# Rounded halves in the expert tiles, first scores moved into the projections, transposes moved up behind the scores

## The chip, the cores and the metric

One Trainium2 chip, of which the kernel uses one core in one launch. The metric is the device time of a launch in microseconds (us). TensorE (PE) multiplies, VectorE (DVE) and GpSimd (POOL) work elementwise and along rows, ScalarE (ACT) evaluates functions and copies, and SyncE (SP) starts DMAs. They run side by side and wait for each other through semaphores.

## The reference

A decoder of two layers runs over `x` (16 batches of 112 rows, width 256) with a context of 16 times 375 rows. Each layer is attention, attention on the context, and a feed-forward part with experts, each with a layer norm ahead and the input added. Everything is float32.

```python
# layer 0
scores = einsum('bhtd,bsd->bhts', q, k1) * scale        # 8 heads of 128, one k and v
probs = softmax(where(causal, scores, finfo.min)); out = (probs @ v1) @ Wo.T
...
q = ln_lat @ Wq; kv = concat([xn, ln_lat]) @ Wkv        # cross attention: 16 heads of 64, 375 + 112 keys
weight = softmax(where(full_mask, einsum('bhld,bhnd->bhln', q * scale, k * scale), neg)); out = (weight @ v) @ Wout
...
expert_idx = argmax(softmax(x @ Wr.T))                  # 8 experts, one per row
inter = gelu(x @ W1[e] + b1[e]); y = inter @ Wo + bo + x; out = layer_norm(y) * gamma + beta
# layer 1
... 16 heads of 64, one k and v, causal; layer_norm(x) times gamma ahead
ctx = (Q @ K.T / dk) @ V                                # context mix: no softmax, so K.T @ V can be made first
x = layer_norm(residual + ctx @ wo + wo_b) * ln_g + ln_b
topv, topi = top_k(softmax(x @ Wg + bg), 2)             # 4 experts, low-rank changes of one shared layer
h = relu(x @ Wi + lora); out = sum_e w_e * (h_e @ Wo)
```

## The kernel before, in words

The order of the work on every engine is written out by hand. Each stage is a block with one function per engine; a semaphore is raised by an instruction when it ends and waited for on the engine that needs it, and each engine takes its instructions strictly in the written order. Nothing moves across the end of a block. Tiles have the stage as a prefix: `l0q`/`l0a` (first attention: projections, then the loop over batches), `l0x` (cross attention), `l0f` (experts of layer 0), `l1a`, `l1x` (context mix), `l1f`.

**l0a.** Projections run in four groups of four batches: eight query products, each in three passes of rounded halves (hi times hi, lo times hi, hi times lo, type fp32r), then k and v. Then, in a new block, each batch goes through `score` on PE (one 112x112 product per head), `softmax` on DVE (add the causal mask, row maximum, shift), `exp` on ACT with the row sums, `invert_sums` on DVE, the division on POOL (`pn`), `transpose_p` on PE, `copy_pT`, `weigh_values`, and `project_out`. The scores of batches 0 and 1 open the block.

**l0x.** A loop over 16 batches, each in eight steps of two heads (`over_steps`: batches 1 to 14 share one loop body). In a step PE makes the scores of its heads from 64 rows of the array (`score`), projections of k and v for later steps or for the next batch, the transposes of the probabilities of the step before (`transpose_p`), and their product with v (`weigh_values`). DVE masks the scores (`mask_score`), copies half of the transposes, inverts the sums, subtracts rounded from full values (the lo halves). ACT does the exponentials, the other half of the copies and the rounded hi halves. POOL divides the probabilities in place.

**l0f.** Rows are routed to experts by a scatter of DMAs on POOL, ahead of which products for the later context mix (`gram`) are made. Then 21 tiles of 128 sorted rows run: `expand` (32 products of 128 columns), gelu on ACT into `hT` (two buffers), and `contract` on PE, 16 products of 256 columns in float32 with `wo`, of width 256, which is resident. Each tile loads 1 MB of weights, three tiles ahead. DVE and POOL normalise the tile's output.

**l1a** is as `l0a` with 16 heads in two halves, k; its block opens with the scores of batch 0 (both halves) and of batch 1. **l1x** takes four groups of four batches: normalise on ACT, transposes, a product with wq, one with the mix of each batch, and one with wo on PE; on DVE the output's statistics, `update` (L2271) and the row statistics; POOL adds biases and takes powers (`add_bias`, `invert_output`). `find_best` on DVE and `subtract_first` on POOL choose the experts of a group two groups later; those of group 2 end the block. **l1f** begins with the transposes of `one_hot` (L2664).

## Time and profile before

| | us |
|---|---|
| median of 3 runs | 1776.1 |
| lowest, highest | 1771.97, 9249.27 |
| profiled execution, its own time | 1779.62 |
| its span, first to last instruction | 1777.8 |

The mean granted clock of TensorE is 0.973 of full speed.

| engine | busy us | share |
|---|---|---|
| PE | 1671.7 | 94% |
| DVE | 1022.1 | 57% |
| ACT | 750.2 | 42% |
| POOL | 530.4 | 30% |

Stages by the timeline: first attention's projections to 74.6 us and its loop to about 211; cross attention about 228 to 1058; routing and first context products to 1111; expert tiles to 1269; context products to 1335; second attention's projections to 1402 and its loop to 1558; context mix to 1640.6; last experts to 1778. A row of the timeline gives the start, the time from start to end of a run of like instructions, the engine, the line, the operation, out<-in, shapes and the count; in brackets stands how long the engine had idled before and what it waited for. Ends of matmuls are modelled, so distances between starts are the safer measure of PE.

### The profile page before, as it was taken

The page shows a single profiled execution, that of the slowest core. Times are in us where ns is not written, and L with a number is a line of the kernel's source. Part 1 is how long each engine was busy: PE and PEld are TensorE (multiplying, and loading weights), DVE is VectorE, ACT ScalarE, POOL GpSimd, SP SyncE. Part 2 cuts the span into 40 slices and gives each one's busy share as a digit, 9 for nine tenths or more (in the row PEclk, how much of TensorE's full clock was granted, in tenths as well). Part 3 has the DMA queues.
Part 4 walks back from the last instruction along what each step waited for, and adds up shares of the span by engine and source line. Part 5 has one row for each costly group of instructions (what it writes and reads, how often), then busy time and mean ns, then how long its engine had stood idle before and what let it go on. Part 6 is the DMA issues. An engine that isn't in the chain of part 4 may idle for free. (4 is left out here: it accounts for less than half of the span.)

```text
span 1777.8 us, 32493 instructions
## 1 busy us (share of the span) xinstructions
PE 1671.7 (94%) x11198; PEld 1323.0 (74%) x11198; DVE 1022.1 (57%) x2461; ACT 750.2 (42%) x2126; POOL 530.4 (30%) x579
## 2 busy tenths in 40 slices
PE   7899899999999999999999987999988799977998
PEld 6687677777777777777777766889877677655666
DVE  5466466655666666566666554142264388757574
ACT  2255344444444444444444430343203477642221
POOL 1022223333333333333333324243420133444000
PEclk9999999999999999999999998999998899987999
DMA  3100300000000000000002004765210000020000
GB/s 99 57 1 1 105 20 11 11 10 10 1 9 10 10 10 10 10 4 6 10 10 63 0 20 154 201 223 187 90 41 20 1 1 1 2 58 1 11 11 21
DMA packets 48805, 67.41 MB, mean 38 GB/s; under 512 B 11826, under 2 KB 42770, under 8 KB 46034
## 3 DMA queue, kind: packets, MB, share of 16 engines
q1 hardware_dynamic: 47186, 62.66, 11.5%
q0 software_dynamic: 1536, 3.67, 0.6%
q8 instruction: 49, 0.80, 0.2%
q14 instruction: 34, 0.28, 0.1%
HBM read 57.02 MB, written 9.31 MB: 37 GB/s over the span
## 5 line engine op out<-in xcount | busy, mean ns | idle before, releaser
L697 POOL TENSOR_TENSOR l0x_p<-l0x_p,l0x_inv 112x488 f32<-112x488 f32 x256 | 251.8, 1005 | 472.6 <-DVE l0x_inv L791 472.6
L900 ACT ACTIVATE l0x_p<-l0x_s,l0x_low 112x488 f32<-112x488 f32 x256 | 178.3, 697 | 275.1 <-DVE l0x_low L780 274.6
L780 DVE CUSTOM_DVE_ANT_0 l0x_s<-l0x_score_ps,l0x_bias 112x488 f32<-112x488 f32 x256 | 160.1, 662 | 113.9 <-PE l0x_score_ps L1040 104.4
L767 DVE TENSOR_TENSOR l0x_kT_lo<-l0x_proj_ps,l0x_kT_hi 128x488 fp32r<-128x488 f32 x128 | 85.3, 667 | 106.3 <-ACT l0x_kT_hi L890 106.3
L1061 PEld LDWEIGHTS l0x_oT_ps<-l0x_pT,l0x_v 122*64 122x64 f32 x2048 | 100.7, 138 | 43.9 <-issue 32.6
L1061 PE MATMUL l0x_oT_ps<-l0x_pT,l0x_v 122*64 122x112 f32 x2048 | 127.9, 267 | 4.9 <-DVE l0x_pT L786 4.1
L1048 PE MATMUL l0x_pT_ps<-ident,l0x_p 112*122 112x112 f32 x1024 | 120.2, 260 | 0.4 <-POOL l0x_p L697 0.3
L1048 PEld LDWEIGHTS l0x_pT_ps<-ident,l0x_p 112*122 112x122 f32 x1024 | 107.0, 138 | 18.2 <-issue 6.0
L996 PE MATMUL l0x_proj_ps<-l0x_kvT_hi,l0x_wkv_hi 128*128 128x488 f32 x256 | 111.0, 434 | 2.9 <-DVE l0x_kvT_lo L755 2.9
L1904 POOL TENSOR_TENSOR l1a_pn<-l1a_p,l1a_inv 112x896 f32<-112x896 f32 x32 | 53.9, 1684 | 190.6 <-DVE l1a_inv L1933 190.6
L1989 ACT ACTIVATE l1a_p<-l1a_p,l1a_shift 112x112 f32<-112x112 f32 x256 | 95.4, 374 | 32.4 <-DVE l1a_shift L1927 32.4
L1005 PE MATMUL l0x_proj_ps<-l0x_wkv_hi,l0x_kvT_hi 128*122 128x512 f32 x256 | 107.0, 418 | 0.0
L1006 PE MATMUL l0x_proj_ps<-l0x_wkv_lo,l0x_kvT_hi 128*122 128x512 f32 x256 | 101.1, 395 | 0.0
L1007 PE MATMUL l0x_proj_ps<-l0x_wkv_hi,l0x_kvT_lo 128*122 128x512 f32 x256 | 101.1, 395 | 0.0
L997 PE MATMUL l0x_proj_ps<-l0x_kvT_lo,l0x_wkv_hi 128*128 128x488 f32 x256 | 99.2, 388 | 0.0
L998 PE MATMUL l0x_proj_ps<-l0x_kvT_hi,l0x_wkv_lo 128*128 128x488 f32 x256 | 99.2, 388 | 0.0
L890 ACT ACTIVATE l0x_kT_hi<-l0x_proj_ps 128x488 fp32r<-128x488 f32 x128 | 72.8, 569 | 35.7 <-PE l0x_proj_ps L998 35.7
L786 DVE COPY l0x_pT<-l0x_pT_ps 122x448 f32<-122x448 f32 x128 | 79.0, 617 | 9.9 <-PE l0x_pT_ps L1048 9.6
L1661 PE MATMUL l0f_hT_ps<-l0f_xsT,l0f_w 128*128 128x128 f32 x672 | 78.5, 275 | 0.0
L1661 PEld LDWEIGHTS l0f_hT_ps<-l0f_xsT,l0f_w 128*128 128x128 f32 x672 | 76.8, 192 | 0.1
L1672 PE MATMUL l0f_y_ps<-l0f_wo,l0f_hT 128*128 128x256 f32 x336 | 75.8, 379 | 0.0
L996 PEld LDWEIGHTS l0x_proj_ps<-l0x_kvT_hi,l0x_wkv_hi 128*128 128x128 f32 x256 | 48.7, 190 | 29.4 <-issue 21.7
(371 smaller groups left out, 3685.8 us busy)
## 6 DMA issues: line engine op xcount, KB each, us to landing
l0f_w<-in_l0f_w SPq DMA_DIRECT2D x21, 1024.0 KB
l0x_c_in<-in_ctx SPq DMA_DIRECT2D x16, 375.0 KB
l1x_gram_context<-in_ctx SPq DMA_DIRECT2D x16, 375.0 KB
sorted_x<-l0x_zeros SPq DMA_DIRECT2D x1, 2816.0 KB, 15.3
l0f_xs<-sorted_x SPq DMA_DIRECT2D x21, 128.0 KB, 2.1
sorted_y<-l0f_ys SPq DMA_DIRECT2D x21, 128.0 KB, 1.7
l0x_wkv<-in_l0x_wkv SPq DMA_DIRECT2D x2, 1024.0 KB, 9.0
x<-in_x SPq DMA_DIRECT2D x4, 448.0 KB, 8.9
```

The costliest lines, as they stand in the source:

```text
L697: nc.gpsimd.tensor_tensor(p[:, i % 2, a, :], p[:, i % 2, a, :], inv[:, i % 2, a:a + 1].broadcast_to([S, KEYS]), ALU.mult).then_inc(pn_read ...
L780: nc.vector.tensor_tensor_reduce(s_sb[:, h % 2, :], score_ps[0:S, h % 2, 0:KEYS], bias[:], -SCALE, 3.4e38, ALU.add, ALU.min, low[:, h:h + ...
L900: nc.scalar.activation(p[:, h // 2 % 2, h % 2, :], s_sb[:, h % 2, :], ACT.Exp, scale=-1.0, bias=low[:, h:h + 1], accum_out=total[:, h:h + ...
L996: nc.tensor.matmul(out, wkv_hi[:, c, at], kvT_hi[:, c, :], start=(c == 0), stop=False)
L997: nc.tensor.matmul(out, wkv_hi[:, c, at], kvT_lo[:, c, :], start=False, stop=False)
L998: done = nc.tensor.matmul(out, wkv_lo[:, c, at], kvT_hi[:, c, :], start=False, stop=(c == KC - 1))
L1005: nc.tensor.matmul(out, kvT_hi[:, c, keys], wkv_hi[:, c, at], start=(c == 0), stop=False)
L1006: nc.tensor.matmul(out, kvT_hi[:, c, keys], wkv_lo[:, c, at], start=False, stop=False)
L1007: done = nc.tensor.matmul(out, kvT_lo[:, c, keys], wkv_hi[:, c, at], start=False, stop=(c == KC - 1))
L1048: done = nc.tensor.transpose(pT_ps[0:KT, a, t * S:(t + 1) * S], p[:, i % 2, a, t * KT:(t + 1) * KT], ident[0:S, 0:S])
L1061: done = nc.tensor.matmul(oT_ps[a * DH:(a + 1) * DH, 0, (i % 4) * S:(i % 4 + 1) * S], v[:, t, (2 * i + a) * DH:(2 * i + a + 1) * DH], pT[: ...
L1661: done = nc.tensor.matmul(hT_ps[:, 2 * (i % 2) + f // 4, (f % 4) * 128:(f % 4 + 1) * 128], w1[:, i % 3, c, f * 128:(f + 1) * 128], xsT[:, ...
```

## The change

1. **First attention:** the scores of batches 0 and 1 are made by PE within the last group of query products (ahead of the first and the fifth product), and batch 0 goes through softmax, exponentials and inversion there; its division opens POOL's next block.
2. **Cross attention:** on PE the transposes of the step before come directly behind the scores. On DVE the copy of the transposes and the inversion come ahead of the splits of queries, values, inputs and keys; on ACT the second exponential and the copy come ahead of the rounding.
3. **Experts of layer 0:** gelu's output goes into one buffer (in the place of `gram_k`), is rounded on ACT (`hT_hi`) and subtracted on DVE (`hT_lo`); `wo` is loaded first and split into halves once (ACT, POOL). `contract` is now 24 products of type fp32r and 256 columns. The third set of expert weights is loaded only when `wo_lo` is made, since `wo` lies in its buffer. The output is scaled in place.
4. **Second attention:** scores of batch 0 move ahead of the last group's query products, with mask, maximum, exponentials and inversion between the copies. `p` becomes two tiles. `wo` is loaded when the loop's block begins. ACT normalises the first four batches for the context mix at the end.
5. **Context mix:** that normalising is gone from its start; POOL adds the next group's bias ahead of `invert_output`; `find_best` and `subtract_first` of group 2 move into the last stage, behind the first result.

What PE's order is at three places, the lines being those of each kernel. Before, the end of the projections of the first attention (`l0q`) and the start of its loop (the three rows of an `L333`-`L335` product stand once):

```order
L333 MATMUL l0a_o_ps<-l0q_xT_hi,l0q_wq_hi 128x448
L334 MATMUL l0a_o_ps<-l0q_xT_lo,l0q_wq_hi 128x448
L335 MATMUL l0a_o_ps<-l0q_xT_hi,l0q_wq_lo 128x448
L343 MATMUL l0a_o_ps<-l0q_xT,l0q_wk 128x448 x2
L347 MATMUL l0a_o_ps<-l0q_wv,l0q_xT 112x128 x8
L180 UNCONDITIONAL_BRANCH
L476 UNCONDITIONAL_BRANCH
L482 MATMUL l0a_score_ps<-l0a_kT,l0a_qT 112x112 x16
L491 MATMUL l0a_score_ps<-ident,l0a_pn 112x112 x8
L500 MATMUL l0a_o_ps<-l0a_pT,l0a_v 128x448 x2
```

After, from the fifth query product of the last group to its sixth, and the end with the start of the loop:

```order
L387 MATMUL l0a_o_ps<-l0q_xT_hi,l0q_wq_hi 128x448
L388 MATMUL l0a_o_ps<-l0q_xT_lo,l0q_wq_hi 128x448
L389 MATMUL l0a_o_ps<-l0q_xT_hi,l0q_wq_lo 128x448
L185 MATMUL l0a_score_ps<-l0a_kT,l0a_qT 112x112 x8
L387 MATMUL l0a_y_ps<-l0q_xT_hi,l0q_wq_hi 128x448
```

And after, the end of that group and the start of the loop:

```order
L389 MATMUL l0a_o_ps<-l0q_xT_hi,l0q_wq_lo 128x448
L397 MATMUL l0a_o_ps<-l0q_xT,l0q_wk 128x448 x2
L401 MATMUL l0a_o_ps<-l0q_wv,l0q_xT 112x128 x8
L221 UNCONDITIONAL_BRANCH
L497 UNCONDITIONAL_BRANCH
L503 MATMUL l0a_score_ps<-ident,l0a_pn 112x112 x8
L512 MATMUL l0a_o_ps<-l0a_pT,l0a_v 128x448 x2
L185 MATMUL l0a_score_ps<-l0a_kT,l0a_qT 112x112 x8
```

Scores now stand in front of the fifth product, and the loop's block opens with the transposes of `l0a_pn`, 8 of them, instead of 16 score products.

In the cross attention, before, the step with keys 0 and 1 of the next batch (scores, one k product of six, transposes, the next):

```order
L1036 MATMUL l0x_score_ps<-l0x_kT_hi,l0x_q_hi 112x488 x2
L1038 MATMUL l0x_score_ps<-l0x_kT_lo,l0x_q_hi 112x488 x2
L1040 MATMUL l0x_score_ps<-l0x_kT_hi,l0x_q_lo 112x488 x2
L996 MATMUL l0x_proj_ps<-l0x_kvT_hi,l0x_wkv_hi 128x488
L997 MATMUL l0x_proj_ps<-l0x_kvT_lo,l0x_wkv_hi 128x488
L998 MATMUL l0x_proj_ps<-l0x_kvT_hi,l0x_wkv_lo 128x488
L996 MATMUL l0x_proj_ps<-l0x_kvT_hi,l0x_wkv_hi 128x488
L997 MATMUL l0x_proj_ps<-l0x_kvT_lo,l0x_wkv_hi 128x488
L998 MATMUL l0x_proj_ps<-l0x_kvT_hi,l0x_wkv_lo 128x488
L1048 MATMUL l0x_pT_ps<-ident,l0x_p 122x112 x8
L996 MATMUL l0x_proj_ps<-l0x_kvT_hi,l0x_wkv_hi 128x488
```

After:

```order
L1046 MATMUL l0x_score_ps<-l0x_kT_hi,l0x_q_hi 112x488 x2
L1048 MATMUL l0x_score_ps<-l0x_kT_lo,l0x_q_hi 112x488 x2
L1050 MATMUL l0x_score_ps<-l0x_kT_hi,l0x_q_lo 112x488 x2
L1058 MATMUL l0x_pT_ps<-ident,l0x_p 122x112 x8
L1006 MATMUL l0x_proj_ps<-l0x_kvT_hi,l0x_wkv_hi 128x488
L1007 MATMUL l0x_proj_ps<-l0x_kvT_lo,l0x_wkv_hi 128x488
L1008 MATMUL l0x_proj_ps<-l0x_kvT_hi,l0x_wkv_lo 128x488
```

The transposes moved from behind the first k product to ahead of it.

In a tile, before:

```order
L1650 MATMUL l0f_xT_ps<-ident,l0f_xs 128x128 x2
L1661 MATMUL l0f_hT_ps<-l0f_xsT,l0f_w 128x128 x16
L1672 MATMUL l0f_y_ps<-l0f_wo,l0f_hT 128x256 x8
L1650 MATMUL l0f_xT_ps<-ident,l0f_xs 128x128 x2
L1661 MATMUL l0f_hT_ps<-l0f_xsT,l0f_w 128x128 x16
```

After (the three rows of a pass repeat eight times):

```order
L1686 MATMUL l0f_xT_ps<-ident,l0f_xs 128x128 x2
L1697 MATMUL l0f_hT_ps<-l0f_xsT,l0f_w 128x128 x16
L1709 MATMUL l0f_y_ps<-l0f_wo_hi,l0f_hT_hi 128x256
L1710 MATMUL l0f_y_ps<-l0f_wo_lo,l0f_hT_hi 128x256
L1711 MATMUL l0f_y_ps<-l0f_wo_hi,l0f_hT_lo 128x256
```

Each float32 product became three of type fp32r.

The diff, cut:

```diff
@@ l0_attention: score, softmax, exp, normalise now stand ahead of the projections @@
+                normalise(pool, 0)
...
+                        if q == Q - 1 and i == 1:
+                            dve.wait_ge(late_w, 32)
+                            softmax(dve, 0)
+                        elif q == Q - 1 and i == 5:
+                            invert_sums(dve, 0)
+                softmax(dve, 1)
...
+                        if q == Q - 1 and i == 0:
+                            score(pe, 0)
+                        elif q == Q - 1 and i == 4:
+                            score(pe, 1)
@@ l0_cross_attention, DVE @@
                     mask_score(b, 2 * i + 1)
+                    if i >= 1:
+                        copy_pT(b, i - 1)
+                    elif not first:
+                        copy_pT(b - 1, HP - 1)
+                    invert_totals(b, i)
                     if i == 0:
                         split_queries(b, 1)
-                        if not first:
-                            copy_pT(b - 1, HP - 1)
...
-                    if i >= 1:
-                        copy_pT(b, i - 1)
-                    invert_totals(b, i)
@@ ACT @@
                     exp(b, 2 * i)
-                    if i == 0:
-                        round_queries(b, 1)
-                    elif i >= 4 and not last:
-                        round_keys(b + 1, 2 * i - 8)
...
                     exp(b, 2 * i + 1)
...
+                    if i == 0:
+                        round_queries(b, 1)
+                    elif i >= 4 and not last:
+                        round_keys(b + 1, 2 * i - 8)
@@ PE @@
                     score(b, i)
...
+                    transpose_p(b, i - 1)
                     if i <= 2:
                         project_high_v(b, 2 * i - 1)
                     elif i >= 4 and not last:
                         project_k(b + 1, 2 * i - 8)
...
-                    transpose_p(b, i - 1)
@@ l0_experts @@
+        wo_hi, wo_lo = ph.sb("wo_hi", [128, FC, D], F32R), ph.sb("wo_lo", [128, FC, D], F32R)
+        wo = w1[:, 2].rearrange("p c (g n) -> p (c g) n", n=D)
...
+                if i == 2:
+                    sp.wait_ge(wo_lo_ready, 2)
...
+            def split_tile(i):
+                for n in range(2):
+                    part = slice(n * FC // 2, (n + 1) * FC // 2)
+                    dve.wait_ge(hT_hi_ready, 2 * i + n + 1)
+                    nc.vector.tensor_tensor(hT_lo[:, i % 2, part], hT[:, part], hT_hi[:, i % 2, part].bitcast(F32),
+                                            ALU.subtract).then_inc(hT_lo_ready, 1)
...
+                    hi, lo = hT_hi[:, i % 2, f, :], hT_lo[:, i % 2, f, :]
+                    nc.tensor.matmul(y_ps[:, i % 2, 0:D], hi, wo_hi[:, f, :], start=(f == 0), stop=False)
+                    nc.tensor.matmul(y_ps[:, i % 2, 0:D], hi, wo_lo[:, f, :], start=False, stop=False)
+                    done = nc.tensor.matmul(y_ps[:, i % 2, 0:D], lo, wo_hi[:, f, :], start=False, stop=(f == FC - 1))
@@ l1_attention @@
+                        if q == Q - 1 and i == 1:
+                            mask_scores(dve, 0, 0, p_even)
+                            find_shift(dve, 0, 0, p_even)
+                            mask_scores(dve, 0, 1, p_even)
+                        elif q == Q - 1 and i == 3:
+                            find_shift(dve, 0, 1, p_even)
+                        elif q == Q - 1 and i == 5:
+                            invert_sums(dve, 0, 0)
+                        elif q == Q - 1 and i == 7:
+                            invert_sums(dve, 0, 1)
...
+                        if q == Q - 1 and i == 0:
+                            exp(act, 0, range(0, 8), p_even)
+                        elif q == Q - 1 and i == 2:
+                            exp(act, 0, range(8, 16), p_even)
...
+                    if q == Q - 1:
+                        pe.wait_ge(act_step, in_step(q, 2))
+                        score(pe, 0, 0)
+                        score(pe, 0, 1)
...
+            def _(sp):
+                sp.dma_start(wo[:], A["l1a_wo"].rearrange("(h p) n -> p h n", p=128)).then_inc(wo_w, 16)
@@ l1_context_mix @@
-                invert_output(g)
                 if g + 1 < G:
                     add_bias(g + 1)
+                invert_output(g)
...
-            subtract_first(G - 2)
...
-            find_best(G - 2)
...
-            normalise(0)
@@ l1_experts, DVE @@
                 if g == 0:
-                    find_best()
+                    find_best(0, G - 2)
+                    find_best(1, G - 1)
```

## Rows read from the trace of the kernel before

**Rows 1.** Stretches: length; PE, PEld, DVE, ACT, POOL busy (count); PE clock; DMA share; GB/s.

```profile
300.00:350.00 50.00, 49.99 (x372) 39.13 (x371) 30.77 (x80) 24.41 (x57) 16.82 (x18) 1.00 0.03 9
1200.00:1250.00 50.00, 50.00 (x348) 46.87 (x347) 12.88 (x28) 18.70 (x63) 19.00 (x34) 1.00 0.57 188
1559.60:1600.00 40.40, 32.40 (x137) 22.93 (x138) 22.39 (x54) 20.51 (x34) 20.79 (x28) 0.78 0.22 64
```

**Rows 2.** What TensorE waited for, whole run: us in total, times, longest.

```profile
PE l1x_o_ps L2403 <- DVE l1x_y L2221: 7.2, 3, 3.2
...
PE l1f_first_hot_ps L2664 <- PEq L2135: 3.9, 1, 3.9
...
PE l1x_xT_ps L2375 <- ACT l0f_x L2308: 3.3, 1, 3.3
```

**Rows 3.** Timeline, start of the first attention: start, us, engine, line, form, count.

```profile
74.61 3.37 PE L482 MATMUL l0a_score_ps<-l0a_kT,l0a_qT 128*112 128x112 f32 x32 [1.47 <-PEq L180]
84.03 1.74 PE L491 MATMUL l0a_score_ps<-ident,l0a_pn 112*112 112x112 f32 x8 [6.05 <-POOL l0a_pn L367]
91.52 0.93 PE L491 MATMUL l0a_score_ps<-ident,l0a_pn 112*112 112x112 f32 x8
```

**Rows 4.** Timeline, TensorE and GpSimd, cross attention of one batch, two steps.

```profile
350.94 0.47 PE L1036 MATMUL l0x_score_ps<-l0x_kT_hi,l0x_q_hi 64*112 64x488 f32 x2
351.79 0.98 PE L1048 MATMUL l0x_pT_ps<-ident,l0x_p 112*122 112x112 f32 x8
352.61 3.62 PE L1070 MATMUL l0x_proj_ps<-l0x_wout,l0x_oT 128*112 128x256 f32 x16
...
350.13 1.96 POOL L697 TENSOR_TENSOR l0x_p<-l0x_p,l0x_inv 112x488 f32<-112x488 f32 x2 [3.51 <-DVE l0x_inv L791]
...
363.89 0.48 PE L1036 MATMUL l0x_score_ps<-l0x_kT_hi,l0x_q_hi 64*112 64x488 f32 x2
364.74 0.49 PE L996 MATMUL l0x_proj_ps<-l0x_kvT_hi,l0x_wkv_hi 128*128 128x488 f32 x1
366.18 0.93 PE L1048 MATMUL l0x_pT_ps<-ident,l0x_p 112*122 112x112 f32 x8
366.88 0.47 PE L996 MATMUL l0x_proj_ps<-l0x_kvT_hi,l0x_wkv_hi 128*128 128x488 f32 x1
368.30 0.40 PE L1005 MATMUL l0x_proj_ps<-l0x_wkv_hi,l0x_kvT_hi 128*122 128x512 f32 x1
```

**Rows 5.** Timeline, expert tiles: TensorE from one tile to the next.

```profile
1201.06 3.74 PE L1661 MATMUL l0f_hT_ps<-l0f_xsT,l0f_w 128*128 128x128 f32 x32
1204.63 3.62 PE L1672 MATMUL l0f_y_ps<-l0f_wo,l0f_hT 128*128 128x256 f32 x16
1208.09 0.38 PE L1650 MATMUL l0f_xT_ps<-ident,l0f_xs 128*128 128x128 f32 x2
```

**Rows 6.** Groups by form: weight loads of the experts; one rounding on ScalarE.

```profile
L1661 PEld LDWEIGHTS l0f_hT_ps<-l0f_xsT,l0f_w 128*128 128x128 f32 x425 | 48.6, 192 | 0.0
...
L876 ACT ACTIVATE l0x_kvT_hi<-l0x_kvT 128x488 fp32r<-128x488 f32 x1 | 0.6, 612 | 0.3 <-DVE l0x_kvT L748 0.3
```

**Rows 7.** The page's group of the exponentials, and the timeline, start of the second attention.

```profile
L1989 ACT ACTIVATE l1a_p<-l1a_p,l1a_shift 112x112 f32<-112x112 f32 x256 | 95.4, 374 | 32.4 <-DVE l1a_shift L1927 32.4
...
1403.10 1.28 ACT L1989 ACT_TABLE_LOAD   x1 [0.27 <-PEq L1775]
...
1407.68 1.04 PE L2019 MATMUL l1a_score_ps<-l1a_kT,l1a_qT 64*112 64x112 f32 x16 [1.28 <-DVE l1a_p L1917]
1414.16 1.71 PE L2031 MATMUL l1a_score_ps<-ident,l1a_pn 112*112 112x112 f32 x8 [5.43 <-POOL l1a_pn L1904]
```

**Rows 8.** Timeline, context mix: VectorE's update beside GpSimd and alone.

```profile
1583.25 3.58 DVE L2271 SCALAR_TENSOR_TENSOR x<-l1x_z,l1x_y_rstd,x 112x256 f32<-112x256 f32 x4
...
1583.19 3.35 POOL L2179 TENSOR_TENSOR l1x_y_in<-l0f_x,l1x_rows 112x256 f32<-112x256 f32 x4
...
1631.34 1.67 DVE L2271 SCALAR_TENSOR_TENSOR x<-l1x_z,l1x_y_rstd,x 112x256 f32<-112x256 f32 x4
```

More of the change, by code:

```diff
@@ L452, in _ @@
             def _(act):
-                def exp(b):
-                    act.wait_ge(softmax_step, b * 4 + 3)
-                    for h in range(H):
-                        done = nc.scalar.activation(p[:, b % 2, h, :], p[:, b % 2, h, :], ACT.Exp, scale=SCALE,
-                                                    bias=shift[:, b % 2, h:h + 1], accum_out=total[:, b % 2, h:h + 1])
-                    done.then_inc(exp_ready, 1)
                 def copy_o(b):
@@ L521, in _ @@
                     if b + 2 < B:
[L522 removed]
+                        score(pe, b + 2)
                     project_out(b, 0)
@@ L1123, in body @@
                         continue
+                    if i >= 4 and last:
+                        route(2 * i - 8)
+                    transpose_p(b, i - 1)
                     if i <= 2:
@@ L1530, in _ @@
             nc.scalar.activation(x1T[:].rearrange("p j c t -> p (j c t)"), xT_ps[:, 0, 0:2 * KC * S], ACT.Copy).then_inc(xT_ready, 1)
+            act.wait_ge(wo_w, 16)
+            for n in range(2):
+                part = slice(n * FC // 2, (n + 1) * FC // 2)
+                nc.scalar.activation(wo_hi[:, part], wo[:, part], ACT.Copy).then_inc(wo_hi_ready, 1)
             def tile_input(i):
```

344 lines of the change are left out of this document (179 added, 165 removed).

## The prediction

> **What bounds the kernel now.** I read the stretches first [rows 1]. In the cross attention PE is busy for 49.99 of 50 us at a full granted clock, and no other engine for more than 30.77; in the expert tiles it is 50.00 of 50. There only fewer or quicker PE instructions save time. The context mix is another case: PE is busy for 32.40 of 40.40 us, at a granted clock of 0.78. Its time is a chain over four engines. The list of PE's waits [rows 2] says where such chains end: 7.2 us on DVE's output rows, 3.9 us on the end of a block, 3.3 us on the first normalising. The timelines give the other two: 6.05 us at the start of the first attention [rows 3], 1.28 and 5.43 us at the start of the second [rows 7].
>
> The sum is made against the profiled execution's own 1779.6 us (its span is 1777.8); the median of the runs is 1776.1, 0.2% less. About 2%, 35.5 us, is what I take as the bound to no change.
>
> **First attention.** The 32 score products cost the same 3.37 us wherever they stand, and their place among the query products waits for nothing. What goes is the 6.05 us in which PE waits for batch 0's mask, maximum, eight exponentials and division [rows 3]; all of that now runs beside the last query products. The division opens POOL's block, but its inputs were ready long before. Next late could be batch 1's transposes: they stood 7.49 us behind batch 0's (84.03 to 91.52), part of it at the halved clock that follows the idle time; without that clock I expect 6.6. Batch 1's exponentials now start when ACT has copied k and v, ahead of the block's start, so its division ends before that. Sum: -6.05 and -0.9, **-7 us**, bounds -9 and -3.
>
> **Cross attention.** No instruction is added or removed; 16 batches of seven steps change order. A step with k products before: scores to k .85 us (363.89 to 364.74), six k products 1.44, transposes .70, six k products 1.42 [rows 4]. After, the transposes follow the scores, as they already do in the step at 350.94: there they take .82 (351.79 to 352.61). Then come six products behind transposes, 1.42, and six more with no change in front of them, some .1 less than 1.44. That is 4.42 against 4.41: nothing. A tenth of a microsecond either way in each of 112 steps is -11 or +11, and I keep these as bounds. DVE and ACT have 19 and 26 us to spare in 50 [rows 1], so their splits may come later; the covers that are thin belong to the transposes, and are a rival below. **0 us.**
>
> **Expert tiles.** A tile takes 7.25 us: 3.57 for the first product (1201.06 to 1204.63), 3.46 for the second (16 instructions, .216 each), .22 for the transposes [rows 5]. The second becomes 24 fp32r products of 256 columns, of which the trace of before has none. From above: an fp32r product of 488 columns takes .24 (six in 1.44 [rows 4]), 24 x .24 = 5.8 us. From below: nothing is known to be quicker than in proportion to columns, 24 x .24 x 256/488 = 3.0, or with .22, what each takes without the six's first, 2.8. Nearest is the float32 product of 128 columns, .112 each (32 in 3.57 [rows 5]): it loads the same 128x128 weights for each product, and shows that such a load, 192 ns by its record [rows 6], does not bind at that pace. 24 x .112 = 2.7. I take 2.8, so -.65 in each of 21 tiles, **-13.5 us**.
>
> By the rows a float32 product costs .84 ns per column (.216/256) and an fp32r product .45 to .49: two to one. The Trainium skill, FP8 and Floating Point Precision, section "TensorE Precision Notes", says that true FP32 takes four passes through the array. The trace disagrees with it as a price: two to one was measured. By four to one, the .216 us of a float32 product would leave .054 for an fp32r one, 1.3 us for the 24, and the sum would be 32 us lower.
>
> Beside PE each tile gains two roundings on ACT, .6 us each [rows 6], and two subtractions on DVE, which I take at .7, as of 512 columns too. In 50 us, some seven tiles, ACT is busy for 18.70 and DVE for 12.88 [rows 1]; with 8.4 and 9.8 more they stay below 28. Contraction waits one tile behind expansion, so the chain gelu, rounding, subtraction has over 3 us of cover. Weights still come 1 MB per tile at a DMA share of .57 in 50 us; 10% more is .63. Ahead of the tiles, `wo` must be loaded and split, which holds ACT's first copies of products by some 4 us and PE by about 1, beside a later wait for the scattered rows; POOL's two subtractions may slow DVE's routing. **+1 us**, bounds 0 and +4. SP's wait ahead of the third weights has two tiles of cover.
>
> **Second attention.** Before, PE waits 1.28 and 5.43 us, and .4 more, until 1414.16 [rows 7]. The waits go, but the exponentials of batch 0 (16 of .374 us on ACT, 6 us, with a read of the sums behind each) and the table load of 1.28 us [rows 7] now stand ahead of ACT's copies of query products, which PE's banks need. I put this at a stall of 2 to 3 us within the projections. `wo`, 1 MB, starts with the loop and is needed some 10 us later. Sum: -7.1 and +3, **-4 us**, bounds -8 and +1.
>
> **Context mix.** The normalising of group 0 leaves the front: 3.3 us waited [rows 2], of which the powers on POOL and a semaphore remain, so -2.1. The four updates on DVE take 3.58 us while POOL adds the bias at the same time (1583.19 and 1583.25), and 1.67 alone [rows 8]. With the bias ahead of the powers they are apart, in three groups: 3 x 1.9 = 5.7 at most, and PE's wait on DVE's rows of 7.2 us [rows 2] bounds what comes back; I take 4. The tail of 3.9 us in front of the last stage [rows 2] keeps about 1: -2.9. The work that left it (about 2.4 us on DVE) lands behind the first result of the last stage, where PE has a group of results in hand. **-9 us**, bounds -3 and -17: the far end is where the granted clock of .78 [rows 1] recovers with the idle time.
>
> **Sum:** -7 + 0 - 13.5 + 1 - 4 - 9 = -32.5: 1747 against 1779.6, and **1743 us** on the median's basis.
>
> **Rivals.**
>
> *A. The halves' weights bind (slower).* If a 256-column fp32r product is paced by its weight load at the recorded .19 us [rows 6], the 24 take 4.56 us against 3.46: +1.1 x 21 = +23, in place of -13.5, and the time is 1780. For it: three loads per block of 128 where there was one. Against: 32 float32 products with loads of 192 ns ran at .112. It decides from .144 us (3.46/24); the whole becomes slower than before from .21 us each. Chance 0.05; of this, with C beside it, 0.02 for over 2% slower.
>
> *B. The transposes come too early in the cross attention.* They stood behind 1.4 us of projections; now the division must end at the scores' end. In the step at 350.94 it ended at 352.09 (350.13 and 1.96), while the transposes began at 351.79, its first head being done [rows 4]: no slack. If DVE's new order makes inversions later by .3 us in two steps of a batch, PE waits .6 x 16 = +10; if in all, over +30. ACT's exponentials come earlier by .5 us in steps with a rounding, which speaks against it. +10 gives 1753; over 33 us in all (2 us a batch) the kernel would be slower than before. Chance 0.17, of which 0.03 slower than before.
>
> *C. The stage gains turn into other waits.* The second attention's projections stall by as much as was saved, and in the context mix PE waits for another engine: 0 and -3 in place of -4 and -9. 1753. For it: a chain over four engines. Chance 0.17.
>
> *D. Clock and chains give more.* PE idles less, the granted clock in the context mix rises from .78, and the halves run at 2.6 us: -17 there, -18 in the tiles, -8 in the cross attention. 1720 to 1735. Chance 0.25.
>
> *E. The four passes of the page* hold after all and an fp32r product of 256 columns takes .054 us: -45 for the tiles, 1711. Chance 0.01.
>
> The forecast as summed has the remaining 0.35. **Range:** it takes in B and C together, 1765, and most of D: 1722 to 1766. **Chances:** over 2% faster means below 1740.6. The forecast lies 2 us above that: a little under half of its share, nearly all of D, E: 0.41. Slower by over 2% (above 1811) needs A and a bad B: 0.03. Within: 0.56.
>
> **What would show it.** Right: no wait of 6 us at the loop's start in the first attention; tiles spaced 6.5 to 6.7 us, `contract` 2.7 to 2.9; distances of 4.4 us from scores through both k products in the cross attention's steps; DVE's updates at 1.7 us in all groups; the last stage about 1 us behind the last products of the mix. Wrong: `pn` or `p` of POOL as releaser of PE's transposes in `l0x`; fp32r products spaced .19; ACT as releaser of the last query products in `l1q`.

## The result, and the profile after

The changed kernel takes 1732.9 us in the median of four runs (1729.86 to 1734.85) against 1774.3; the ratio is 0.9769, 95% interval 0.9746 to 0.9793, so 41 us or 2.3% faster, just past 2%. Of the four runs of the kernel before, one took 9249.27 us; the ratio goes by the other three. The forecast was 1743, the range 1722 to 1766. The profiled execution took 1729.9 us (span 1727.4), and that of before 1779.6: they lie 3.0 and 5.4 us from their medians, away from each other, so the two traces differ by 50 us. TensorE's mean granted clock rose from 0.973 to 0.987.

Starts of the same rows in the two traces give the stages (us). The forecast's terms stand beside them.

| stretch | before | after | difference | forecast |
|---|---|---|---|---|
| to the first transposes of `l0a_pn` | 84.03 | 78.33 | -5.7 | |
| to the first scores of the cross attention | 148.26 | 146.02 | -2.2 | -7 with the row above |
| cross attention | 829.17 | 819.42 | -9.8 | 0 |
| routing and first context products | 50.92 | 49.87 | -1.1 | +1 |
| expert tiles | 156.92 | 145.84 | -11.1 | -13.5 |
| second context products | 68.07 | 67.67 | -0.4 | |
| second attention, to its first transposes | 76.79 | 69.56 | -7.2 | |
| its loop, to the first transposes of the mix | 147.61 | 146.05 | -1.6 | -4 with the row above, and -2.1 for the mix's front |
| context mix, to the first transposes of `one_hot` | 79.15 | 67.52 | -11.6 | -6.9 |

The stretches of the changed kernel, as in [rows 1]: length; busy time and count of PE, PEld, DVE, ACT and POOL; the granted clock; DMA share; GB/s.

```profile
300.00:350.00 50.00, 50.00 (x388) 39.26 (x387) 33.15 (x81) 23.93 (x56) 18.41 (x19) 1.00 0.03 9
1111.00:1262.00 151.00, 141.85 (x1148) 137.85 (x1147) 78.26 (x144) 73.80 (x204) 68.36 (x106) 1.00 0.59 184
1522.00:1560.00 38.00, 32.32 (x161) 22.06 (x162) 22.12 (x63) 19.97 (x33) 20.73 (x30) 0.96 0.23 68
```

PE still fills the cross attention. In the tiles DVE and ACT are now busy about half the time. In the first part of the mix the granted clock is far above the .78 of [rows 1].

What PE waited for after the change, in us in total, times and longest (before in [rows 2]):

```profile
PE l0f_xT_ps L1686 <- DMA l0f_xs<-sorted_x: 5.6, 3, 3.4
...
PE l0x_oT_ps L1071 <- ACT l0x_pT L916: 5.0, 6, 2.0
...
PE l1x_o_ps L2458 <- DVE l1x_y L2278: 5.0, 5, 1.8
...
PE l1a_o_ps L2098 <- DVE l1a_pT L2019: 2.2, 1, 2.2
...
PE l1x_xT_ps L2430 <- PEq L1994: 1.2, 1, 1.2
```

The 6.0 us of `l0a_pn` are gone from the list, the 3.9 of the last stage's start are down to .9, and the 3.3 of the mix's front became 1.2, the change of blocks. DVE's rows still cost 5.0. `weigh_values` waits for its copies of the transposes by 5.0 and .9 us (it was 4.1), and the tiles' transposes for `xs`, a DMA, by 5.6 (it was 4.2).

The timelines of the changed kernel follow, each with a row's start, its time from start to end, engine, line, form, count and, in brackets, the idle time before it. The start of the first attention's loop (in [rows 3] it waited 6.05 us there):

```profile
78.33 0.95 PE L503 MATMUL l0a_score_ps<-ident,l0a_pn 112*112 112x112 f32 x8 [1.47 <-PEq L221]
```

One step of the cross attention (in [rows 4] the transposes stood between the k products):

```profile
353.60 0.47 PE L1046 MATMUL l0x_score_ps<-l0x_kT_hi,l0x_q_hi 64*112 64x488 f32 x2
354.45 0.98 PE L1058 MATMUL l0x_pT_ps<-ident,l0x_p 112*122 112x112 f32 x8
355.21 0.47 PE L1006 MATMUL l0x_proj_ps<-l0x_kvT_hi,l0x_wkv_hi 128*128 128x488 f32 x1
357.95 0.40 PE L1015 MATMUL l0x_proj_ps<-l0x_wkv_hi,l0x_kvT_hi 128*122 128x512 f32 x1
...
360.36 0.48 PE L1046 MATMUL l0x_score_ps<-l0x_kT_hi,l0x_q_hi 64*112 64x488 f32 x2
```

Scores to transposes is .85, transposes to the first k product .76, and both k products take 2.74; the next scores come 6.76 behind the last ones, 6.82 before ([rows 4] has one of these starts, 363.89; the next was 370.71).

Two expert tiles, from transposes to the next tile's:

```profile
1163.50 0.38 PE L1686 MATMUL l0f_xT_ps<-ident,l0f_xs 128*128 128x128 f32 x2
1163.71 3.74 PE L1697 MATMUL l0f_hT_ps<-l0f_xsT,l0f_w 128*128 128x128 f32 x32
...
1170.16 0.38 PE L1686 MATMUL l0f_xT_ps<-ident,l0f_xs 128*128 128x128 f32 x2
```

6.66 us between them in place of 7.25 [rows 5]. The DMAs that bring a tile's input were late three times, though:

```profile
1120.79 0.44 PE L1686 MATMUL l0f_xT_ps<-ident,l0f_xs 128*128 128x128 f32 x2 [3.36 <-DMA l0f_xs<-sorted_x]
...
1128.71 0.44 PE L1686 MATMUL l0f_xT_ps<-ident,l0f_xs 128*128 128x128 f32 x2 [1.04 <-DMA l0f_xs<-sorted_x]
...
1136.77 0.44 PE L1686 MATMUL l0f_xT_ps<-ident,l0f_xs 128*128 128x128 f32 x2 [1.18 <-DMA l0f_xs<-sorted_x]
```

The second attention, from the last k product to the first product with v:

```profile
1370.02 1.77 PE L1982 MATMUL l1a_o_ps<-l1q_x1T,l1q_wk 128*128 128x448 f32 x4 [0.88 <-ACT l1a_qT L1925]
...
1376.71 0.98 PE L2089 MATMUL l1a_score_ps<-ident,l1a_pn 112*112 112x112 f32 x8 [0.40 <-DVE l1a_p_odd L1827]
1377.94 0.95 PE L2089 MATMUL l1a_score_ps<-ident,l1a_pn 112*112 112x112 f32 x8 [0.25 <-POOL l1a_pn L2006]
1381.10 2.76 PE L2098 MATMUL l1a_o_ps<-l1a_pT,l1a_v 112*64 112x448 f32 x8 [2.20 <-DVE l1a_pT L2019]
```

The k product waits .88 us for ScalarE's copies (before it idled for .76 there), and the 5.43 of [rows 7] are gone. A new wait of 2.20 us stands ahead of the product with v: DVE has batch 1's scores to mask and their maxima to find before it copies the transposes.

The context mix: DVE's updates, and the start of the last stage:

```profile
1543.11 1.67 DVE L2328 SCALAR_TENSOR_TENSOR x<-l1x_z,l1x_y_rstd,x 112x256 f32<-112x256 f32 x4
...
1556.14 1.67 DVE L2328 SCALAR_TENSOR_TENSOR x<-l1x_z,l1x_y_rstd,x 112x256 f32<-112x256 f32 x4 [0.93 <-POOL l1x_y_rstd L2244]
...
1590.28 0.94 PE L2725 MATMUL l1f_first_hot_ps<-ident,l1f_one_hot 112*80 112x112 f32 x4 [0.88 <-PEq L2193]
```

The updates take 1.67 us where [rows 8] has 3.58.

### The profile page after: what moved, and what is told of

It is laid out like the page before. It is cut to its first block and busy times, and to the rows that moved or that the text cites. A ratio compares the mean times of both kernels' runs of the same rounds, so it can differ in the third digit from the quotient of the medians.

```text
span 1727.4 us, 32951 instructions
## 1 busy us (share of the span) xinstructions
PE 1637.9 (95%) x11366; PEld 1307.8 (76%) x11366; DVE 1066.8 (62%) x2503; ACT 774.1 (45%) x2170; POOL 545.3 (32%) x581
## 5 line engine op out<-in xcount | busy, mean ns | idle before, releaser
L707 POOL TENSOR_TENSOR l0x_p<-l0x_p,l0x_inv 112x488 f32<-112x488 f32 x256 | 261.9, 1044 | 433.0 <-DVE l0x_inv L801 431.8
L1058 PEld LDWEIGHTS l0x_pT_ps<-ident,l0x_p 112*122 112x122 f32 x1024 | 98.9, 138 | 45.3 <-issue 38.7
L1058 PE MATMUL l0x_pT_ps<-ident,l0x_p 112*122 112x112 f32 x1024 | 126.3, 266 | 0.7 <-POOL l0x_p L707 0.6
L1006 PE MATMUL l0x_proj_ps<-l0x_kvT_hi,l0x_wkv_hi 128*128 128x488 f32 x256 | 104.0, 406 | 2.8 <-DVE l0x_kvT_lo L765 2.8
L2006 POOL TENSOR_TENSOR l1a_pn<-l1a_p_even,l1a_inv 112x896 f32<-112x896 f32 x16 | 26.9, 1685 | 137.4 <-POOLq L1853 98.6
L211 ACT ACTIVATE l0a_p<-l0a_p,l0a_shift 112x112 f32<-112x112 f32 x128 | 47.8, 375 | 45.9 <-DVE l0a_shift L201 45.6
L916 ACT ACTIVATE l0x_pT<-l0x_pT_ps 122x448 f32<-122x448 f32 x128 | 66.9, 523 | 1.8 <-PE l0x_pT_ps L1058 1.8
L218 POOL TENSOR_TENSOR l0a_pn<-l0a_p,l0a_inv 112x896 f32<-112x896 f32 x16 | 27.0, 1684 | 120.4 <-DVE l0a_inv L206 120.4
## 6 DMA issues: line engine op xcount, KB each, us to landing
sorted_x<-l0x_zeros SPq DMA_DIRECT2D x1, 2816.0 KB, 16.1
```

What stands on the lines that cost most here:

```text
L707: nc.gpsimd.tensor_tensor(p[:, i % 2, a, :], p[:, i % 2, a, :], inv[:, i % 2, a:a + 1].broadcast_to([S, KEYS]), ALU.mult).then_inc(pn_read ...
L1006: nc.tensor.matmul(out, wkv_hi[:, c, at], kvT_hi[:, c, :], start=(c == 0), stop=False)
L1058: done = nc.tensor.transpose(pT_ps[0:KT, a, t * S:(t + 1) * S], p[:, i % 2, a, t * KT:(t + 1) * KT], ident[0:S, 0:S])
```

## Experiments

There are twelve experiments, one of them the changed kernel once more. The table gives medians, the ratio to the kernel before on the same chip with its 95% interval, and three stretches of each profile as in the table above (us).

| kernel | median | ratio | cross attention | tiles | mix |
|---|---|---|---|---|---|
| only the first attention's part | 1765.5 | 0.9945 (0.9925 to 0.9965) | 827.66 | 156.82 | 76.62 |
| only the cross attention's part | 1764.7 | 0.9927 (0.9899 to 0.9955) | 820.84 | 158.81 | 75.22 |
| only the second attention's part | 1769.5 | 0.9963 (0.9947 to 0.9979) | 829.16 | 154.64 | 73.58 |
| whole change without the tiles' part | 1737.8 | 0.9775 (0.9746 to 0.9805) | 819.42 | 154.83 | 67.51 |
| whole change, once more | 1731.5 | 0.9762 (0.9739 to 0.9786) | 819.44 | 146.18 | 65.83 |
| whole change with the old mix and last experts | 1742.9 | 0.9816 (0.9789 to 0.9844) | 824.15 | 145.48 | 75.16 |
| before, with PE's new order alone | 1792.0 | 1.0095 (1.0075 to 1.0114) | 848.76 | 159.00 | 75.21 |
| before, with DVE's and ACT's new order alone | 1774.3 | 0.9994 (0.9976 to 1.0012) | 829.80 | 158.62 | 79.13 |
| transposes behind both k products | 1740.8 | 0.9802 (0.9780 to 0.9824) | 830.61 | 146.43 | 65.21 |
| tile products in halves of columns | 1772.9 | one run | 819.42 | 191.32 | 65.21 |
| bias behind the powers | 1739.6 | 0.9795 (0.9763 to 0.9828) | 819.43 | 146.02 | 71.56 |
| contexts loaded later | 1721.2 | 0.9688 (0.9670 to 0.9706) | 820.47 | 139.61 | 66.69 |

### The parts one by one

Three kernels take the functions of one part from the changed kernel, and the rest from the one before. For the second attention's a wait in the experts, on the number of its loads, had to follow:

```diff
-                    act.wait_ge(next_w_w, 96)
+                    act.wait_ge(next_w_w, 16 * len(next_w.loads(A)))
```

> The first attention's part alone, on the kernel before. Theory (each part gives its own stage's time and the parts add up): the first transposes of l0a_pn start at 78.3 us as in the changed kernel, against 84.03 before, the cross attention's first row 7 us earlier, and the whole is 7 us shorter (ratio 0.996); the later stages are as before. Rival (part of the 41 to 50 us comes from an earlier phase shifting the clock or DMAs of later stages): more than 12 us in all, with later stages shorter too.

Measured: the first transposes start at 78.14 us and the cross attention's first scores at 224.05, 8.2 us earlier than before; ratio 0.9945, 10 us. The interval (6 to 13 us) holds both the expected 7 and the rival's 12, so the whole time does not decide between them. The profile is 14.1 us shorter than that of before. Beyond the 8.2, stages whose code is the old one are shorter: 1.5 in the cross attention, 2.1 in the second attention up to its transposes, and 2.5 in the context mix (76.62, where the trace of before has 79.15). The first of these is all in the first batch, and the granted clock is another there; the stretches are the first batch here and in the profile of before:

```profile
224.05:273.01 48.96, 46.56 (x353) 36.19 (x352) 31.42 (x78) 24.14 (x56) 18.32 (x19) 1.00 0.01 3
232.29:282.78 50.49, 48.09 (x355) 37.22 (x354) 31.42 (x78) 24.20 (x56) 18.34 (x19) 0.97 0.01 3
```

So the part's own gain is the 8.2, and what the rival spoke of is there too, though its size in the whole is not settled.

> The cross attention's part alone, on the kernel before. Theory: a batch falls from 51.67 to 51.20 us between like rows, in every batch, 7.5 us in all (ratio 0.996). Rival (it was the better state in which the stage is entered, or the shorter stage before it): 51.67 us a batch as before and no change of time.

Measured: 51.20 us a batch, 820.84 for the stage, and 0.9927. The shorter batch does not hang on the stage before it, and the rival is out. The expected 0.996 lies outside the interval all the same: the profile is 12.4 us shorter than that of before, of which 8.3 are in this stage and 3.9 in the context mix, whose code is the old one.

> The second attention's part alone (the context mix and the last experts are the old ones, so the four batches are normalised again there). Theory: from the first query product to the last row of the output product 5 us less (in the changed kernel 212.2 became 207.4), and 4 to 5 us in the whole. Rival (the gain of the changed kernel there was the clock's, which was higher by chance of the phase before): under 2 us, with query products at .57 us at the start as before.

Measured: 69.64 us to the first transposes where it was 76.79, but 149.34 for the loop where it was 147.61: 5.4 us less together, and 0.9963, 6.6 us. So part of what the moved softmax saves comes back as a longer loop.

### The tiles' part undone

The changed kernel with the old `l0_experts`, and the wait above.

> The changed kernel with the old experts of layer 0: wo and gelu's output in float32, 16 products of 256 columns. Theory: the tiles are spaced 7.25 us again in place of 6.66, so it is 11 to 12 us longer than the changed kernel (about 1744 where that has 1732.9, ratio to before 0.983). Rival (DMAs and not PE bounded the tiles, or the split of wo ahead of them cost as much as it saved): under 6 us longer.

Measured: the tiles take 154.83 us where the whole change has 145.84, 146.18 and 146.02 in three profiles, so the part is worth 9 us there, with routing .8 shorter without it. Over all, the old tiles took 154.6 to 159.0 us in seven profiles, the new ones 145.5 to 146.4 in five that have them unchanged. The tiles are 7.25 us apart again (1193.11 to 1200.35), but they waited for `xs` by only 2.4 us (4.2 in the profile of before), against 5.6 and 4.7 in the two profiles of the whole change: part of what a quicker tile saves is spent waiting for DMAs, and the expected 11 to 12 us did not come. The expected ratio of 0.983 lies outside the interval. In whole time the two medians differ by 6.3 us but come from different chips, and their ratios, 0.9775 and 0.9762, do not tell them apart, so that the rival's "under 6 us" is not excluded there. The stage shows the gain; its size in the whole is not settled.

### The whole change once more, and the old mix

> The changed kernel once more, on the chip of the three runs beside it, as their measure. Theory: ratio 0.977, the stages as in its first profile within what they vary; the context mix, from its first transposes to the last stage's first, 67.5 us again. Rival (that length was one lucky profile, since the same old code took 73.6 to 79.2 us in four profiles): 70 us or more.

Measured: 0.9762, and 65.83 us for the mix. Its short length was no lucky profile.

The next kernel is the changed one with the old `l1_context_mix` and `l1_experts`.

> The changed kernel with the old context mix and the old last experts. Theory: that stretch has 74 to 79 us in place of 67.5, and its front 3.35 us instead of 1.24, so 8 to 14 us longer than the whole change. Rival (it is shorter because the stages before it leave the clock high): within 4 us of the whole change.

Measured: 75.16 us for the mix in place of 65.83, and 3.35 for its front in place of 1.24, 11.4 us together; 1742.9 against 1731.5 on the same chip, also 11.4, or 9.6 by the ratios. The two profiles differ by 16.1, though, of which 4.7 are in the cross attention, whose code is the same: all its middle batches take 51.20, but its last ran at a granted clock of .91 in place of 1.00, and from 1038 to 1043 us at .50. The old mix took 73.6 to 79.2 us in seven profiles, the new one 65.2 to 67.5 in six that have it unchanged, so the old one's length of 79.15 in the profile of before was at the long end of its own spread.

By their medians and ratios the five parts are worth some 10, 13, 7, 6 and 11 us, 47 together, where the whole change gave 41 to 44. Each of the five is uncertain by 3 to 5 us, so they neither show nor exclude that the parts add up.

### Which engine's order saves in the cross attention

The first kernel takes from the changed one only TensorE's block of `l0_cross_attention`, the second only the other engines' blocks.

```diff
                     score(b, i)
...
+                    transpose_p(b, i - 1)
                     if i <= 2:
                         project_high_v(b, 2 * i - 1)
                     elif i >= 4 and not last:
                         project_k(b + 1, 2 * i - 8)
...
-                    transpose_p(b, i - 1)
```

> The kernel before with TensorE's new order in the cross attention alone; VectorE and ScalarE keep the old one. Theory (what is saved is TensorE's own: one switch less between float32 and fp32r products in each step): the full 51.20 us a batch, if the division is in time, else up to 1 us more by waits for p in the first steps. Rival (the gain is an unseen wait that the other engines' order removes): 51.6 or more.

Measured: 52.53 us a batch and 1.0095, 17 us slower. The theory gave 51.20, and at most 52.20 if the division came late, and fell here; the rival, which spoke of an unseen wait, had the number but not the reason. Steps 4 to 7 take 6.76, 6.76, 8.52 and 6.75 us, as in the changed kernel, so what TensorE's order saves there is its own. Step 0 takes 6.45 in place of 5.86, step 1 5.56 in place of 5.47, and step 2 5.58 in place of 4.93. The last batch, with 61.5 in place of the 55.3 of before, loses 6 us more, at a granted clock of .86 in place of .97. Step 0, in the timeline:

```profile
335.96 0.48 PE L1036 MATMUL l0x_score_ps<-l0x_kT_hi,l0x_q_hi 64*112 64x488 f32 x2
336.81 0.98 PE L1048 MATMUL l0x_pT_ps<-ident,l0x_p 112*122 112x112 f32 x8
337.63 1.95 PE L982 MATMUL l0x_proj_ps<-l0x_kvT,l0x_wq 128*128 128x112 f32 x16
...
341.50 0.99 PE L1061 MATMUL l0x_oT_ps<-l0x_pT,l0x_v 122*64 122x112 f32 x16 [0.52 <-DVE l0x_pT L786]
342.42 0.48 PE L1036 MATMUL l0x_score_ps<-l0x_kT_hi,l0x_q_hi 64*112 64x488 f32 x2
```

and in the waits of that kernel:

```profile
PE l0x_oT_ps L1061 <- DVE l0x_pT L786: 20.9, 33, 2.4
```

The transposes are done at once, but `weigh_values` waits for DVE's copy: in the old order DVE takes the split of the queries first. It is this wait, not the division (.8 us in all), that comes of TensorE's order alone.

> The kernel before with VectorE's and ScalarE's new order in the cross attention alone; TensorE keeps the old one. Theory: 51.67 us a batch as before, or a tenth less. Rival: 51.3 or less, since an unseen wait goes.

Measured: 51.67 us a batch, and 0.9994. The side order saves nothing by itself and is what makes the other one pay.

### What the place behind the scores saves

In the changed kernel, for steps 4 to 7 of all batches but the last:

```diff
-                    transpose_p(b, i - 1)
+                    if i < 4 or last:
+                        transpose_p(b, i - 1)
...
                         project_k(b + 1, 2 * i - 7)
+                        transpose_p(b, i - 1)
```

> The changed kernel with the cross attention's transposes of steps 4 to 7 moved behind the second k product, ahead of v, so that a float32 piece stands between two fp32r pieces again. Theory (what the new place saved is one switch between kinds of products): these steps take 6.81 to 6.82 us again in place of 6.76, the others 5.86, 5.48, 4.94, 6.14 as in the changed kernel, 4 us in all. Rival (any place that is not between two passes of a product is as good): 6.76.

Measured: 6.78, 6.87, 8.90 and 6.80 us in these steps, against 6.76, 6.76, 8.52 and 6.75; the others as expected. 51.77 us a batch, .57 more in place of some .24. The theory's 6.81 to 6.82 came in none of the four steps, though step 7 is near, and the rival's 6.76 in none either, so this run does not decide between them. One such step:

```profile
398.92 0.48 PE L1046 MATMUL l0x_score_ps<-l0x_kT_hi,l0x_q_hi 64*112 64x488 f32 x2
...
399.76 0.49 PE L1006 MATMUL l0x_proj_ps<-l0x_kvT_hi,l0x_wkv_hi 128*128 128x488 f32 x1
...
402.53 0.93 PE L1058 MATMUL l0x_pT_ps<-ident,l0x_p 112*122 112x112 f32 x8
...
403.23 0.47 PE L1015 MATMUL l0x_proj_ps<-l0x_wkv_hi,l0x_kvT_hi 128*122 128x512 f32 x1
...
405.70 0.48 PE L1046 MATMUL l0x_score_ps<-l0x_kT_hi,l0x_q_hi 64*112 64x488 f32 x2
```

Scores to the k product .84, transposes .70, then v. The price of a run of products depends on what stands before it and behind it, and the rows say by how much. A k product's first pass takes .33 behind scores or .31 behind transposes, and .22 behind its like. The transposes take .76 behind scores and .70 behind k, as long as k or v follows. In the old order both k products began with a long pass (.11 and .09 more), in the new one only one (.09), and the transposes cost .06 more: .05 less by the sum, .06 measured. In this kernel the long pass is there twice again, at k and at v (1.56 us for v's six in place of 1.49), and the transposes are back at .70: .04 more by the sum. Steps 4 and 7, longer by .02 and .05, fit that. Step 5 is .11 longer, and the .38 of step 6 lie ahead of its query product and behind it, by these distances as waits; so most of this kernel's loss has another cause. That the saving is one of neighbours is argued from the rows, and no run shows it by itself.

### What paces an fp32r product of 256 columns

```diff
-                    nc.tensor.matmul(y_ps[:, i % 2, 0:D], hi, wo_hi[:, f, :], start=(f == 0), stop=False)
...
+                    for n in range(2):
+                        at = slice(n * 128, (n + 1) * 128)
+                        nc.tensor.matmul(y_ps[:, i % 2, at], hi, wo_hi[:, f, at], start=(f == 0 and n == 0), stop=False)
...
```

> The changed kernel with each of the 24 products of a tile's output made as two of 128 columns, 48 in all, so the same columns with twice the weight loads. Theory (a product of 256 columns is paced by its weight load, .120 us): each of 128 columns takes .11 to .12, the 48 take 5.3 to 5.8, and a tile 9.1 to 9.5 us in place of 6.66. Rival (paced by columns, .47 ns each): the 48 take 2.9 to 3.1 us and a tile 6.7 to 6.9.

Measured: 1772.9 us in one run, and 9.12 us a tile:

```profile
1241.82 0.41 PE L1686 MATMUL l0f_xT_ps<-ident,l0f_xs 128*128 128x128 f32 x2
...
1242.06 3.74 PE L1697 MATMUL l0f_hT_ps<-l0f_xsT,l0f_w 128*128 128x128 f32 x32
...
1245.55 0.31 PE L1711 MATMUL l0f_y_ps<-l0f_wo_hi,l0f_hT_hi 128*128 128x128 f32 x1
...
1250.94 0.40 PE L1686 MATMUL l0f_xT_ps<-ident,l0f_xs 128*128 128x128 f32 x2
```

The transposes take .24 of it, the first product 3.49, and the 48 5.39, at .111 from start to start. Half the columns, nearly the same time: a product of 128 columns is not paced by its columns. This run doubles the number of products along with the loads of weights, so by itself it does not tell the two apart. Other rows of the changed kernel speak for the weights. Float32 products with weights of 128x112 stand .098 apart whether they have 8 columns, 64 or 112; the eight of 8 columns, for example, are

```profile
1014.34 0.95 PE L1094 MATMUL l0x_proj_ps<-l0f_wr,l0x_x1T 128*112 128x8 f32 x8
```

Those with weights of 128x128 and 112 columns stand .112 apart (L992). So the floor moves with the width of the weights and not with the columns. A product of 256 columns takes .120, so it stands at about the place where columns begin to count.

### The bias in the context mix

```diff
+                invert_output(g)
                 if g + 1 < G:
                     add_bias(g + 1)
-                invert_output(g)
```

> The changed kernel with GpSimd's old order in the context mix: invert_output, then the next group's bias. Theory: VectorE's updates of the first three groups take 3.58 us again in place of 1.67, its statistics come 1.9 us later, and the stretch from the first transposes of the mix to the last stage's first is 4 to 6 us longer than 67.5. Rival (the stretch was shortened by the tail and front that were taken away): at most 2 us longer.

Measured: 71.56 us for the mix, 4.0 to 6.3 more than the profiles with the new order; median 1739.6. DVE's updates of groups 0, 1 and 3 (group 2's took 3.58 too):

```profile
1545.51 3.58 DVE L2328 SCALAR_TENSOR_TENSOR x<-l1x_z,l1x_y_rstd,x 112x256 f32<-112x256 f32 x4
...
1559.38 3.58 DVE L2328 SCALAR_TENSOR_TENSOR x<-l1x_z,l1x_y_rstd,x 112x256 f32<-112x256 f32 x4
...
1590.52 1.67 DVE L2328 SCALAR_TENSOR_TENSOR x<-l1x_z,l1x_y_rstd,x 112x256 f32<-112x256 f32 x4
```

and TensorE's waits for its rows:

```profile
PE l1x_o_ps L2458 <- DVE l1x_y L2278: 7.0, 3, 3.2
```

So the order of two instructions on GpSimd carries about half of what the mix gained. The rest of the stretch is its tail (3.88 to .88) and what the clock gives back; the clock has its share in these 4.0 to 6.3 us too, since it was .85 in this mix and .90 to .94 in those with the new order.

### Contexts loaded later

The stretches of the changed kernel's profile show the DMAs all but full (share .95, .86) while the tiles begin, and TensorE busy for only 6.64 us of the second 10 (columns as above):

```profile
1105.00:1115.00 10.00, 10.00 (x90) 10.00 (x90) 5.45 (x11) 5.85 (x18) 6.10 (x10) 1.00 0.95 218
1115.00:1125.00 10.00, 6.64 (x59) 6.43 (x57) 3.30 (x6) 3.58 (x12) 3.13 (x6) 1.00 0.86 258
```

```diff
-                if i < 4:
-                    load_context(EARLY + i)
+                if 10 <= i < 14:
+                    load_context(EARLY + i - 10)
```

> The changed kernel with the DMAs of four contexts, 375 KB each, started at tiles 10 to 13 in place of 0 to 3, where the DMA engines were full (share 1.01 from 1105 to 1115 us). Theory: TensorE's waits for xs, 5.6 us in the changed kernel's profile, fall to 2 or less, and the whole to 3 or 4 us below it (ratio to before .975). Rival (weights of 1 MB a tile at the start are enough to fill the DMAs): waits of 4 us and more, no change.

Measured: no wait for `xs` at all, and every tile 6.67 us from the next:

```profile
1117.50 0.38 PE L1686 MATMUL l0f_xT_ps<-ident,l0f_xs 128*128 128x128 f32 x2
...
1124.17 0.38 PE L1686 MATMUL l0f_xT_ps<-ident,l0f_xs 128*128 128x128 f32 x2
```

The tiles take 139.61 us in place of 145.8 to 146.2, and the whole 1721.2 us, ratio 0.9688 (0.9670 to 0.9706). That is 0.7% below the changed kernel's median and 0.8% below its ratio, which come from other chips, and more than the 3 to 4 us expected. The two profiles differ by 6.1 us in all, and the tiles by 6.2; where the rest of the medians' difference lies no profile shows. This version beats both kernels. The same two stretches of it:

```profile
1105.00:1115.00 10.00, 10.00 (x90) 10.00 (x90) 5.47 (x11) 5.62 (x17) 5.86 (x10) 1.00 1.06 305
1115.00:1125.00 10.00, 10.00 (x89) 10.00 (x88) 5.79 (x10) 5.86 (x17) 3.37 (x6) 1.00 0.59 187
```

The first is as full as in the changed kernel (a share above 1 comes of counting a packet's whole time where it starts), but the second is at .59, and TensorE is busy throughout.

## Why the prediction was right

It said 1743, -32.5 us; measured were -41 by the medians, with the same sign and inside the range. By its chances a change within 2% was the likelier outcome (0.56), and 2.3% faster, to which it gave 0.41, came. By the stages of the two profiles the change is -50.6 us, and there every term but that of the tiles gave more than was forecast. That the median lies nearer to the forecast than the profiles do is no merit of the sum: these two profiles lie away from their medians, on opposite sides. Its terms:

**First attention, -7.** Right: -5.7 and -2.2, and -6.1 and -2.2 in the second profile of the whole change; alone, 8.2 up to the same place. The 6.05 us went, and the transposes follow the last projections with nothing in between but the change of blocks. Batch 1's transposes stand 6.19 behind batch 0's, where 6.6 was forecast.

**Cross attention, 0.** This term was mis-sized. The 14 middle batches take 51.20 us in place of 51.67, -6.6. Of the -9.8, 1.6 are in the first batch and are not the order's: with either order it took 48.9 to 49.1 where the granted clock in it was 1.00, and 49.9 to 51.8 where it was .97. The last batch took 53.74 in place of 55.33, another -1.6, with a granted clock of 1.00 in place of .97; how much of that is the order's, no run separates.

The method was right and one of its numbers was not. The price of transposes behind scores was read at 351.79 as .82, in a step in which a float32 product comes next; ahead of an fp32r product it is .76. It is not a wait for the division, of which the rival B speaks at the same rows. In the changed kernel the same step takes .82 again, though the division ends at 341.47, ahead of the transposes:

```profile
339.51 1.96 POOL L707 TENSOR_TENSOR l0x_p<-l0x_p,l0x_inv 112x488 f32<-112x488 f32 x2 [3.47 <-DVE l0x_inv L801]
...
341.55 0.98 PE L1058 MATMUL l0x_pT_ps<-ident,l0x_p 112*122 112x112 f32 x8
342.38 3.62 PE L1080 MATMUL l0x_proj_ps<-l0x_wout,l0x_oT 128*112 128x256 f32 x16
```

The second k product behind the first was counted as 1.34 and is 1.32. .85 + .76 + 1.42 + 1.32 is 4.35, against 4.41. Steps 4 to 7 save .05 to .07 each, .24 a batch; steps 0 and 1 save .04 and .06. Step 2 saves .15, of which the forecast knew nothing: .12 of it are between the products that transpose the next batch's input and `weigh_values`, which before began .16 us behind the end of DVE's copy of the transposes (350.03 and 349.87). By these rows it is a short wait for that copy, too short for the list of waits; no run tests it alone.

**Tiles, -13.5.** The second product took 2.95 us, .120 from start to start, where 2.8 was taken, and the first .08 less than before (3.49), so a tile 6.66 in place of 6.60. That makes -12.4 over 21 tiles, and 1.4 more was lost where tiles waited for DMAs: -11.1. The forecast had set the DMA share by a late stretch, .57, and the tiles' beginning is at .95 and .86; contexts loaded later showed that. The rival E did not happen: a float32 product took .216 and an fp32r one of the same 256 columns .120; with 448 columns they are .376 and .20. The Trainium skill, FP8 and Floating Point Precision, section "TensorE Precision Notes", says that true FP32 takes four passes through the array, and no run here shows four as a ratio of times.

**Routing, +1.** -1.1 in the two profiles. Over all, it took 48.9 to 50.9 us in seven profiles without the tiles' part and 49.6 to 52.0 in seven with it, so a cost of about 1 is neither shown nor excluded.

**Second attention, -4.** -5.4 alone, and -6.7 in the table (-7.2 and -1.6, less the 2.1 of the mix's front). The term that was mis-sized is the stall of 2 to 3 us in the projections: ACT's copies were late by .88 alone; in its place a wait of 2.20 stands at the loop's start.

**Context mix, -9.** -13.7 in the two profiles (-11.6, and -2.1 at its front), of which the long mix in that of before is part; -11.4 against the old mix on the same chip. The mechanism was right: updates at 1.67, shown by putting GpSimd's order back. The clock gave more than was taken: .96 from 1522 to 1560 and .83 from 1560 to 1590, where it was .78 and .79 in the two halves before.

**The rivals.** A is out: a product with weights of 128x128 goes at .111, and A decides from .144. B did not happen in the whole change, where the page's group of the transposes has them waiting for the division for .6 us in all:

```profile
L1058 PE MATMUL l0x_pT_ps<-ident,l0x_p 112*122 112x112 f32 x1024 | 126.3, 266 | 0.7 <-POOL l0x_p L707 0.6
```

It was right in that a cover was thin, though another one: with DVE's and ACT's order left as it was, TensorE's new order made the kernel 17 us slower, by the copies and not by the division. C did not happen, though a piece of it did, in the loop of the second attention. D is nearest to what came, 1732.9 within its 1720 to 1735. Of its -8 in the cross attention 6.6 came by the order and more by the clock, and most of its -17 in the mix came; its -18 in the tiles did not.

## What to carry to other kernels

A price read from start to start belongs to the neighbours of its row: the same eight transposes took .70, .76 or .82 us by what stood before and behind them. Take it from a row with the neighbours that the new order will have, above all where the difference is multiplied by a hundred steps. An order on the engine that bounds pays only if the engines that serve it are turned round with it; the half of such a change can be slower than none. After a change that shortens each step, look again at the DMAs' share where they are fullest, not at the mean.

## What the runs showed of the hardware

- VectorE's update of four 112x256 rows took 3.55 to 3.59 us while GpSimd added rows of the same size, and 1.67 alone, in all fourteen profiles.
- With weights of 128x128 an fp32r product took .111 us with 128 columns, .120 with 256 and .22 with 488; a float32 product .112 with 128 and .216 with 256. With weights of 128x112 a float32 product took .098 with 8, 64 or 112 columns.
- The same old code of the context mix took 73.6 to 79.2 us in seven profiles, and the granted clock was .78 in one and .86 in another of them. A single profile is no measure of a stretch whose engines wait for each other.
- The first batch of the cross attention took 48.9 us at a granted clock of 1.00 and 50.5 at .97, both with the old order; its last took 53.7 at 1.00 and 57.4 at .91 with the new one.
